# A two-block transformer on one core: setup spread between turns, a LayerNorm's scale and shift inside the Gelu, and a new order of stages

## The reference

```
x = x + window_attention(_ln_c(x))         # 12 heads, windows of 8x8 shifted by 4, relative position bias
t = t + bitlinear_ffn(_ln_t(t))            # weights sign(W - mean of group), activations scaled by a maximum over images
x = x + deformable_attention(_ln_c(x))     # q, grouped 3x3 conv, LayerNorm(ln_g, ln_b), Gelu, offsets, tanh,
                                           # bilinear sampling, k and v, softmax over 256 tokens
t = t + moe(_ln_t(t))                      # 4 experts, the best 2 of each token, Gelu
```

```
t = (t - mu) / jnp.sqrt(var + LN_EPS) * ln_g + ln_b
t = jax.nn.gelu(t, approximate=False)
offset = jnp.tanh(t @ w_offp) * offset_range
```

## Time and profile before

| | |
|---|---|
| three runs | 1073.13, 1075.67, 1384.31 us |
| median | 1075.67 us |
| the profiled execution, whole | 1075.66 us |
| its span, first to last instruction | 1073.9 us |
| PE busy | 870.6 us, 81% of the span |
| DVE busy | 645.4 us, 60% |
| ACT busy | 581.2 us, 54% |
| POOL busy | 286.4 us, 27% |
| mean granted clock of TensorE | 0.924 of full speed |

### The profile page before, as it was taken

How to read it: one execution, slowest core, us unless ns; L and a number is a source line. 1 busy time by engine, 2 the same in 40 slices (tenths; PEclk the granted TensorE clock), 3 DMA queues, 4 the chain that set the end, 5 groups by cost and what they waited for, 6 DMA issues and landing times.

```text
span 1073.9 us, 25725 instructions
## 1 busy us (share of the span) xinstructions
PE 870.6 (81%) x9272; PEld 581.1 (54%) x9318; DVE 645.4 (60%) x2053; ACT 581.2 (54%) x1241; POOL 286.4 (27%) x610
## 2 busy tenths in 40 slices
PE   0257888888875656688999999999999999999887
PEld 0035555555553444444765765666576576565556
DVE  1247777777663723447657865865875686685433
ACT  0136766766753611265476467457547646744653
POOL 5046666666630000122022012112201201220100
PEclk9999999999986955686999998999999899998989
DMA  4100000000000003331231242133123213213000
GB/s 118 21 10 12 18 15 12 17 15 12 10 10 8 8 2 97 100 92 48 62 101 49 57 100 71 39 95 86 51 67 103 56 48 102 71 45 87 5 5 8
DMA packets 40082, 51.90 MB, mean 48 GB/s; under 512 B 23097, under 2 KB 27242, under 8 KB 40010
## 3 DMA queue, kind: packets, MB, share of 16 engines
q1 hardware_dynamic: 40010, 50.93, 18.4%
HBM read 44.51 MB, written 6.40 MB: 47 GB/s over the span
## 4 chain that ended last, share of the span: by engine, by line
PE 39%; DVE 18%; issue 16%; ACT 10%; POOL 9%; DMA 5%; SPq 2%; DVEq 0%; ACTq 0%; POOLq 0%
PE ps L1276 33%; DVE nm L946 4%; PE ps L1281 4%; DMA haty<-hat_scratch 3%; ACT prob L1235 2%; DVE haty L929 2%; POOL srstd L539 2%; ACT y1all L1136 1%; DVE acc L1016 1%; POOL rh L573 1%; SPq L380 1%; DVE b_xn L746 1%; ACT stackt L1073 1%; POOL rh L572 1%; PE ps L1569 1%
## 5 line engine op out<-in xcount | busy, mean ns | idle before, releaser
L1276 PE MATMUL ps<-stackt 53*64 53x64 bf16 (+3 forms) x2304 | 135.1, 229 | 37.7 <-ACT prob L1235 21.5
L1073 ACT COPY stackt<-ps 128x768 bf16<-128x768 bf16 x192 | 144.0, 805 | 40.0 <-PE ps L1281 39.8
L946 DVE TENSOR_REDUCE nm<-ps 128x2 f32<-128x512 f32 x192 | 123.2, 683 | 36.3 <-PE ps L1276 36.1
L1260 ACT ACTIVATE hb<-ps 128x512 f32<-128x512 f32 (+1 forms) x128 | 62.9, 492 | 146.0 <-PE ps L1276 145.0
L929 DVE TENSOR_TENSOR haty<-haty,hatx 128x512 f32<-128x512 f32 x96 | 64.2, 686 | 114.7 <-DMA haty<-hat_scratch 113.9
L1276 PEld LDWEIGHTS ps<-stackt 53*64 53x64 bf16 (+3 forms) x2304 | 49.8, 105 | 131.4 <-ACT prob L1235 70.1
L1276 PE MATMUL ps<-b_xnt,we 128*128 128x256 f32 x384 | 112.9, 403 | 3.6 <-ACT hb L1260 3.3
L539 POOL TENSOR_TENSOR prstd<-pveps,neghalf 128x2 f32<-128x2 f32 x48 | 34.1, 711 | 301.4 <-DVE pveps L741 294.4
L1235 ACT ACTIVATE prob<-ps 128x512 f32<-128x512 f32 x192 | 104.8, 602 | 8.4 <-PE ps L1276 7.4
L1276 PE MATMUL ps<-we,hb 128*128 128x96 f32 x768 | 97.2, 276 | 0.5 <-ACT hb L1260 0.5
L539 POOL TENSOR_TENSOR srstd<-sveps,neghalf 128x2 f32<-128x2 f32 x32 | 31.7, 990 | 243.8 <-DVE sveps L741 243.8
(11 more groups left out here) (243 smaller groups left out, 1573.0 us busy)
## 6 DMA issues: line engine op xcount, KB each, us to landing
haty<-hat_scratch SPq DMA_DIRECT2D x64, 384.0 KB
hatx<-hat_scratch SPq DMA_DIRECT2D x32, 384.0 KB
hat_scratch<-hat SPq DMA_DIRECT2D x32, 96.0 KB
xraw<-x_scratch SPq DMA_DIRECT2D x17, 96.0 KB, 15.7
out<-acc SPq DMA_DIRECT2D x16, 96.0 KB, 16.4
we<-in_we SPq DMA_DIRECT2D x1, 768.0 KB
y1all<-in_x SPq DMA_DIRECT2D x16, 48.0 KB, 1.7
y1all<-in_x SPq DMA_DIRECT2D x32, 24.0 KB, 2.1
```

The costliest lines, as they stand in the source:

```text
L946: v.tensor_reduce(nm[:, t, a, 2 * pq:2 * pq + 2], ps[:, 2 + a, :].rearrange("p (b n) -> p b n", n=TOK), AX.X, ALU.max, negate=True).then_i ...
L1073: return a.copy(stackt[:, x, :, P * t:P * t + P], bank_bf(bank))
L1260: a.activation(hb[:, e % 2].rearrange("p m n -> p (m n)")[:, 2 * TOK * k:2 * TOK * k + n_], ps[:, 6, 0:n_], ACT.Gelu).then_inc(S("c_h"), 1)
L1276: return m.matmul(o, l, r, start=start, stop=stop)
```

## The change

Nothing of what is computed changes. Seven edits:

1. **Setup between turns.** The loads are put in four groups. Images 1 and 2 are loaded first on SP, around the five constants of the bias; six constants of pass A's first steps are loaded on ACT's queue (`loads_first`); the others follow on SP, those of pass C in turn 2. The engines no longer wait for the whole setup. `run_straight` has a table `before` of setup pieces that are issued ahead of a turn: on POOL the clearing of the stacks inside turn 1, two rows ahead of turn 2, the rest ahead of turn 5; on DVE `signs_setup` ahead of turn 3; on PE `sums_setup` and on ACT `bias_setup` ahead of turn 3; on SP `bias_rows` ahead of turn 6.
2. **Norm scale and shift within the Gelu.** `lng` and `lnb` become columns. PE transposes the normalised `tn` at once, and one Gelu on ACT reads the transposed values out of PSUM with scale and bias per partition and writes `tnt`. L908, L909, the Gelu on `tn` and the plain copy are gone.
3. **One division** for both tiles in pass C.
4. **The kept sum on POOL**: `kept(i)` is copied by POOL after `power`.
5. **Casts merged**: `copies` has two instructions with a repeated source instead of four.
6. **A new `ORDER_C`.**
7. The warming matmuls of pass A read `onesb` instead of `bias3`.

```diff
-ORDER_C = "aaokakoaaaoboeboaesbaesbokeoeabsebeobssesaoeboeessabooaes"
+ORDER_C = "aaokaaoaaoboebasoesbkkaoeobeebaoebesbossesaobeesseabooaes"
...
-        def run_straight(eng, order, behind, **parts):
+        def run_straight(eng, order, behind, before, **parts):
             last = max(behind.values())
             for j in range(1, IMAGES + last + 1):
+                if j in before:
+                    before[j]()
                 turn_of(order, {c: p(j - behind[c]) for c, p in parts.items() if 1 <= j - behind[c] <= IMAGES})
...
+            load_x(1)
+            load(loads_bias, bt_dma)
+            load_x(2)
+            load(loads_ffn, ffn_in)
+            sp.wait_ge(setup_act, ACT_TABLE)
...
+            run_straight(sp, ORDER_A, BEHIND_A, {2: load_last, 6: bias_rows}, ...)
...
+            run_straight(pool, ORDER_A, BEHIND_A, {2: rows_setup, 5: last_setup}, ...)
...
                 power("p", "a_rstd")
                 yield
+                if i == 1:
+                    stacks_setup()
...
                 power("p", "c_rstd")
+                w("xadd", 1)
+                g.tensor_copy(kept(i), xin[:]).then_inc(S("c_kept"), 1)
...
-            dve.wait_ge(weights_in, 16 * len(loads))
-            dve.wait_ge(setup_pool, PZERO)
+            dve.wait_ge(first_in, 16 * len(loads_first))
...
+            run_straight(dve, ORDER_A, BEHIND_A, {3: signs_setup, 4: bias_ready, 8: last_setup}, ...)
...
-                v.tensor_copy(kept(i), xin[:])
...
-                own.link(normed("p", tn, both(tiles(0, C))))
-                own.link(v.tensor_tensor(tn[:], tn[:], row(lng), ALU.mult))
-                v.tensor_tensor(tn[:], tn[:], row(lnb), ALU.add).then_inc(S("c_cn"), 1)
+                normed("p", tn, both(tiles(0, C))).then_inc(S("c_cn"), 1)
...
-                for t in range(TILES):
-                    w("otr", t + 1)
-                    divide(own, t, 4 + t).then_inc(S("c_on"), 1)
+                w("otr", 2)
+                divide(own, 4).then_inc(S("c_on"), 1)
...
+            for t, name in loads_first:
+                act.dma_start(t[:], A[name]).then_inc(first_in, 16)
...
-                    a.copy(d[:, :, HD * b:HD * b + HD], one)
-                    ins = a.copy(d[:, :, HD * (b + 2):HD * (b + 2) + HD], one)
+                    ins = a.copy(d, one.to_broadcast([P, TILES * HEADS, 2, HD]))
...
-                a.activation(tn[:], tn[:], ACT.Gelu).then_inc(S("c_cg"), 1)
                 yield
                 w("tt", 1)
-                a.copy(tnt[0:C, :], ps[0:C, 0, 0:TOK]).then_inc(S("c_tnt"), 1)
+                a.activation(tnt[0:C, :], ps[0:C, 0, 0:TOK], ACT.Gelu, bias=lnb[:, 0:1], scale=lng[:, 0:1]).then_inc(S("c_tnt"), 1)
...
+            def sums_setup():
+                pe.wait_ge(setup_act, ACT_TABLE)
+                pe.wait_ge(setup_dve, DVE_SUM1)
```

More of the change, by code:

```diff
@@ L536, in power, with rows_setup, last_setup @@
+            def rows_setup():
+                for t in (b_xnt, ont):
+                    setup(g.memset(t[:], 0.0))
+            def last_setup():
+                for t in (xst, tnt, qpad, xz, bias3, cbias3):
+                    setup(g.memset(t[:], 0.0))
+                setup(g.memset(y2all[:, QIMG, :], 0.0))
             def power(half, ready):
@@ L721, in _ @@
-            setup(v.tensor_tensor(bres[:], be2[:], bpart[:, 0, :], ALU.subtract))
-            setup(v.tensor_copy(bpart[:, 1, :], bres[:]))
-            setup(v.tensor_tensor(bpart[:, 2, :], bres[:], bpart[:, 1, :], ALU.subtract))
-            dve.wait_ge(setup_act, 4)
-            setup(v.tensor_scalar(ebz[:], ebz[:], 8.0, 8.0, ALU.mult, ALU.add))
-            setup(v.tensor_scalar(lscale[:], lscale[:], math.log(100.0), None, ALU.min))
-            setup(v.memset(xst[C:C + 1, :], 1.0))
-            assert n[0] == DSETUP
+            assert n[0] == DVE_FIRST
@@ L965, in attend_c @@
                 w("proj", 1)
+                w("kept", 1)
                 w("acc", -1)
@@ L1041, in setup @@
                 act.wait_ge(setup_act, n[0])
-            act.wait_ge(setup_pe, 3)
-            setup(a.activation(hid_t[:], ps[:, 1, 0:REL], ACT.Relu, bias=cpb_b1[:, 0:1]))
-            act.wait_ge(setup_pe, 4)
-            setup(a.copy(bt_sb[:], ps[0:HEADS, 2, 0:REL]))
-            act.wait_ge(setup_pe, 5)
-            setup(a.activation(ebz[:, 0:6], ps[:, 3, 0:384].rearrange("p (h n) -> p h n", n=WIN), ACT.Tanh, scale=0.5))
-            setup(a.activation(ebz[:, 6:12], ps[:, 4, 0:384].rearrange("p (h n) -> p h n", n=WIN), ACT.Tanh, scale=0.5))
@@ new lines, in _, with bias_setup @@
+            setup(a.activation(hid_t[:], ps[:, 4, 0:REL], ACT.Relu, bias=cpb_b1[:, 0:1]))
+            act.wait_ge(setup_pe, PE_TABLE)
+            setup(a.copy(bt_sb[:], ps[0:HEADS, 5, 0:REL]))
+            act.wait_ge(setup_dve, DVE_FIRST)
+            setup(a.activation(lscale[:], lscale[:], ACT.Exp))
+            assert n[0] == ACT_SCALE
+            def bias_setup():
+                act.wait_ge(setup_pe, PE_FLIP)
+                setup(a.activation(ebz[:, 0:6], ps[:, 6, 0:384].rearrange("p (h n) -> p h n", n=WIN), ACT.Tanh, scale=0.5))
+                setup(a.activation(ebz[:, 6:12], ps[:, 7, 0:384].rearrange("p (h n) -> p h n", n=WIN), ACT.Tanh, scale=0.5))
+                assert n[0] == ACT_TANH
+                act.wait_ge(setup_dve, DVE_BIAS)
+                setup(a.activation(expbias[:], ebz[:].rearrange("p (b a) n -> p a b n", a=2), ACT.Exp))
+                setup(a.activation(w1s[:], w1s[:], ACT.Sign))
+                setup(a.activation(w2s[:], w2s[:], ACT.Sign))
+                assert n[0] == ACT_SIGN
@@ L1295, in _ @@
[L1295 to L1303 removed]
+            pe.wait_ge(bt_dma, 16 * len(loads_bias))
```

257 lines of the change are left out of this document (135 added, 122 removed).

## The result

The changed kernel takes **1041.24 us** (median of 4 runs, 1040.25 to 1042.68) against 1074.99 for the kernel before on the same chip, a ratio of 0.9693 with a 95% interval of 0.9672 to 0.9713. One of the four runs of the kernel before took 1384.31 us and is left out of that ratio; the median of its other three is 1074.32. The forecast was 1033, its range 1022 to 1051. The profiled execution has a span of 1040.9 against 1073.9, so 33.0 us went where 43.0 were expected. The table divides the difference over the stretches of the kernel. It marks them by one repeated row: ACT's copy of `f_xnt`, once a turn in pass A, and PE's product with `wo`, once a turn in pass C from its turn 4 on.

The account below looks back on a forecast made before the run. It took 50 us at the start as pure waiting and pass C's loop as PE-bound, its second half tied to DVE. Span 1073.9 - 28.6 (setup) - 3.3 - 1.2 - 0.4 - 9.5 = 1030.9, hence 1033 us, range 1022 to 1051.

Parts of the forecast that it names:

- The start: Setup: image 1 loads first, so PE's first product of pass A moves from 52.83 to 11.5, minus 41.3 us.
- Turn 3: Pass A: setup work put ahead of this turn on DVE, then ACT, is covered by nothing, plus 10.8 us.
- POOL's clearings ahead of turn 5: Pass A: 2.5 us of clearings against about 1.7 us of POOL's idle time in a turn, plus 1.0 us.
- Casts: Pass A: two merged casts on ACT for four save 0.22 us in each of 15 turns, minus 3.3 us.
- Pass C, filling: Pass C's first turn loses scale, shift and Gelu from its chain, minus 1.2 us; turns 2 to 4 give 0.
- The loop: Pass C: PE's waits shrink by 0.79 us a turn over 12 turns, period 37.1, minus 9.5 us.
- the ring: Pass C's loop: DVE from hatx to hat 21.5 plus DRAM 15.4 makes 36.9 us, fitting with 0.2 to spare.
- the hidden 0.37: Pass C's loop: PE's wait for a DVE maximum inside a group of four score matmuls, 0.37 us, would go.
- the 0.20 for the split maxima: Pass C's loop: PE's wait of 0.20 us for DVE's split maxima would go.
- Draining: Pass C, turns 17 to 20: they gain the merged casts twice, minus 0.4 us.
- The new order as part of the loop's gain: Pass C's loop: under the new order both PE waits for DVE go, 0.57 us a turn.
- the unmoved loop: Rival, pass C: PE's waits merely move, the loop stays at 37.9 us a turn, total 1042; chance 0.22.

Follow-up runs that it names:

- Run 1: Changed kernel with POOL's clearings of the two stacks and va issued at its start instead of behind its first root; 1034.45 us, ratio 0.9606.
- run 5: Changed kernel with the setup part from ahead of turn 3 put ahead of turn 2, on the same engines; 1031.79 us, ratio 0.9603.
- Run 6: Kernel of Run 1 with POOL's other clearings, from ahead of turns 2 and 5, put in turn 1; 1031.81 us, ratio 0.9606.
- run 9: Kernel before with three extra unused matmuls a turn of pass C at PE's wait for the first exponential; 1068.47 us, ratio 0.9931.
- run 10: Changed kernel, ranks left in place, with three extra unused matmuls a turn at PE's wait for the first exponential; 1035.00 us, ratio 0.9617.
- run 8: Changed kernel with DVE's ranking one step earlier and three extra unused matmuls a turn at PE's longest wait; 1028.93 us, ratio 0.9562.
- run 3: Changed kernel with the old order string of pass C, all else as changed; 1040.34 us, ratio 0.9677.
- run 7: Changed kernel with pass C's kept copy back on DVE, ahead of its statistics; 1040.40 us, ratio 0.9702.
- runs 10 to 12: After run 10: changed kernel with all gaining edits, 1017.26 us; then the same without the earlier ranks and with pass C's old order, 1023.67 us.

## Why the prediction was right, and where its sum was off

The direction, the main mechanism and the range were right: the gain comes from the start, pass C gives a third of it, and turn 3 gives back 11. The forecast's own range of 1027 to 1039 was missed by 2. Luck is in the total too: 4 of the 33 us are falls of the clock that the kernel before had in draining and the changed one had not, and 2.7 went the other way in the loop. The sum was off by 10.0 us of span, in these steps:

- **The start, -41.3 forecast, -36.2 measured.** This step failed. I let POOL's clearings run "from about 9.2 to 17" and checked them only against POOL's own next work. That part was right (the roots started at 22.54, the clearings' end was 18.35). What I did not check was DVE beside them. Run 1 shows that they cost the 5.1 us: without them the product stands at 11.58 for 11.5. That this is so close is in part luck. The constants reached DVE some 1.5 us later than I had said, and PE's warming matmuls, behind which the product follows there without a wait, just covered it. The Trainium skill (SBUF — State Buffer, Who interferes with whom) says that a DVE instruction in a two-port mode and GpSimd exclude each other on a shared port, and that the one that issues first has it for its whole instruction. The 5.96 against 0.63 agrees, and goes further: the longer of the two norm instructions took 5.91 by itself, through three clearings and not one. I had weighed this rule for a copy of 0.3 us and not for clearings of 2.66 each.
- **Turn 3, +10.8 forecast, +11.5 measured.** Right, and run 5 shows the reasoning behind it: where POOL's roots cover it, the same work costs 5.4.
- **POOL's clearings ahead of turn 5, +1.0 forecast, +2.4 measured.** I counted their time on POOL less its idle time. What I left out is again DVE beside them: a cast of 2.23 us instead of 0.20. Run 6 takes 3.9 us out of the stretch (35.7 in run 1, 31.8 in run 6); how much of it is the cast and how much POOL's own time was not taken apart.
- **Casts, -3.3 forecast in pass A.** This step failed, in the path more than in the price. Two casts hold ACT for 0.83 where four held it for 1.01, so 0.18 is saved for a forecast of 0.22, and the loop gained these 0.18. A turn of pass A gained only 0.04. I had said that ACT's queue there leads straight to the sums of squares. In the changed kernel's chain ACT waits 0.21 between two of its writes of `y1all` behind the casts (from 124.46 on), and in the turn at 136.98 the chain leaves ACT and goes through POOL's split of q and k (L565 to L574). That these two took up the rest is my reading; no run tested it. The -1.1 of that row of the table is 0.06 in each of ten turns, one turn of 16.33 in the kernel before, and 0.2 in pass B.
- **Pass C, filling, -1.2 forecast, -0.1 measured.** Not tested. In these turns PE's mean granted clock is 0.5 to 0.8 in both kernels, and the new Gelu on ACT takes 0.56 where the copy took 0.37, which gives back 0.2 in turn 1.
- **The loop, -9.5 forecast, -5.7 measured.** With PE's wait filled in both kernels (runs 9 and 10), which keeps the clock full but for the first turn, the twelve turns take 455.7 and 447.3, that is -8.5: the mechanism and nearly its size. The other 2.7 of the shortfall are clock falls, of which this execution of the changed kernel had more. Within the -8.5 two readings failed. First the ring: I reckoned 36.9, "it fits, with 0.2 us to spare". Its way through DRAM I put at 15.4 by taking `hatx` to arrive 37.88 after 708.29. The trace before has that arrival at 746.53, which makes the way 15.75 and the ring 37.25, over the period of 37.1 that I forecast:

```profile
746.53 0.69 DVE L929 TENSOR_TENSOR haty<-haty,hatx 128x512 f32<-128x512 f32 x1 [6.52 <-DMA haty<-hat_scratch]
```

  Nor was it "15.4 each time": the other turns of the loop before have 14.0 to 15.9. With the earlier ranks the loop takes 444.7 (run 8), so the ring cost 2.6 us. Second, the hidden 0.37 in a group of scores did not go whole: 0.16 of it stays even in undisturbed turns (0.56 for 0.40), and the 0.20 for the split maxima goes without the new order too (run 3). Against that, the undisturbed turn is 0.9 shorter than before, more than the forecast 0.79.
- **Draining, -0.4 forecast, -4.3 measured.** By the traces this is not the change: the kernel before spent some 7 and some 10 us at half clock in these turns, the changed kernel none. With PE's wait filled the kernel before takes 119.5 for them (run 9), the changed one 119.0 as it is and 120.0 in run 10.
- **The kept copy at 0** (run 7) held. **The new order as part of the loop's gain** held in its direction: 0.2 us a turn as it stands, 0.4 with the earlier ranks (runs 10 to 12). With the casts at 0.18 some 0.3 of the 0.9 us a turn are left; how they divide between the fused Gelu and the one division was not taken apart.

Of the rivals, the unmoved loop would have given 1042, a number near the measured one and for the wrong reason: the loop did move, by 0.5 to 0.9 in each undisturbed turn. The scores did not fall far behind the convolution (their hidden wait shrank), and `hatx` took 0.7 longer than reckoned in the ring shown, far from the 3.6 a turn that would have made the kernel slower.

## What to carry to other kernels

When work moves on GpSimd, look at what VectorE does in the same microseconds, not only at what GpSimd does next: a clearing that is free for its own engine held a 0.6 us norm for 6 us, and GpSimd had 7.5 idle microseconds ahead of it. Read the length of a transfer that closes a ring from its own two ends and from all turns, not from the period, since the longest ones set the period as soon as the slack is smaller than their spread. When an instruction on the chain gets shorter, look for the next chain right behind it: 0.18 us less on ScalarE gave 0.04 a turn. And before a time is put down to an edit, or to none, count the turns at a lower clock in both traces: two falls more in the changed kernel than in run 3 hid what the new order gives.

## What the runs showed of the hardware

- **With a wait of 0.9 us on PE filled, the clock stayed full.** In the kernel with the earlier ranks the granted clock fell from full (2.4 GHz) to half (1.2 GHz) in every third turn of the loop, for about 7 us. Stretches of 2 us around one fall (length, PE busy, count, granted clock, DMA share, GB/s):

```profile
590.00:592.00 2.00, 2.00 (x18) 1.00 0.03 6
592.00:594.00 2.00, 0.98 (x8) 1.00 0.31 92
594.00:596.00 2.00, 2.00 (x23) 0.86 0.19 12
596.00:598.00 2.00, 2.00 (x16) 0.50 0.36 111
```

  What PE did before it fell was to idle 0.92 us, with 0.48 five microseconds earlier. The same pattern in the two turns between left the clock alone. With three matmuls of 512 columns in the gap the falls were gone from the second turn of the loop on, in all five kernels with this edit, whatever their order and setup. A single fall had cost 1.7 to 1.8 us. Whether the matmuls would do the same at another place in the turn was not run.
- **One VectorE instruction was held through several GpSimd instructions**, not through one. One norm instruction took 5.91 us beside clearings of 2.66, 2.66 and 0.74. The cast of 2.23 us in turn 5 ended at 84.46, behind the last (ending at 84.41) of the five clearings from 82.17 on, which follow one another on GpSimd with no gap.
- **A float32 norm of 2 x 96 columns has several prices**, by what GpSimd does beside it: 0.57 in pass A, 0.73 in the loop before beside a cast, 0.83 in the changed loop beside a copy and a subtraction, 1.05 beside the split in run 7, 5.96 beside clearings.
